# One cosine product between every four attention products in a graph-attention kernel

## The reference, cut to what matters

```
h     = relu(layernorm(x))
deg   = clip(adj.sum(axis=1), 1);  dis = deg ** -0.5
diff  = (dis[:, None] * adj * dis[None, :]) @ h - h
sim   = h @ h.T / (|h_i| |h_j|)
attn  = softmax(beta * sim * adj, axis=1)
out   = x + diff + sigmoid(alpha) * (attn @ h - h)
```

## Time and profile before

| | |
|---|---|
| median of three runs | 1919.48 us (1919.47 to 1920.07) |
| the profiled execution's own time | 1921.04 us |
| its span, first to last instruction | 1919.1 us |
| TensorE busy | 1827.4 us, 95% |
| ScalarE, GpSimd, VectorE busy | 1306.8, 1269.1 and 1226.5 us |
| mean granted TensorE clock | 0.991 |

### The profile page before, as it was taken

The page is one execution under the profiler, slowest core; times in us unless marked ns, Lnnn a source line. Parts: engine busy times, 40 slices in busy tenths (PEclk is TensorE's granted clock), DMA queues, the critical chain, the costliest instruction groups (busy, mean ns, idle before and its releaser), DMA issues.

```text
span 1919.1 us, 44747 instructions
## 1 busy us (share of the span) xinstructions
PE 1827.4 (95%) x19602; PEld 1408.7 (73%) x19602; DVE 1226.5 (64%) x1382; ACT 1306.8 (68%) x1262; POOL 1269.1 (66%) x792
## 2 busy tenths in 40 slices
PE   0489999999999999999999999999998999999998
PEld 0366777777777777777777777777777888888887
DVE  6887787787778778777877877787775210111111
ACT  7688898889889888988988898899887000000000
POOL 3099999999999999999999999999883000000000
PEclk9699999999999999999999999999999999999999
DMA  9639887767888877778888767888426755554530
GB/s 177 97 63 135 106 106 101 100 89 102 100 106 101 108 105 89 100 96 100 106 100 109 100 89 100 100 107 100 116 92 239 226 178 182 170 200 165 202 107 12
DMA packets 188455, 229.38 MB, mean 120 GB/s; under 512 B 9316, under 2 KB 164964, under 8 KB 183396
## 3 DMA queue, kind: packets, MB, share of 16 engines
q0 software_dynamic: 135168, 67.13, 45.1%
q1 hardware_dynamic: 25060, 144.71, 20.6%
q10 hardware_dynamic: 28032, 14.69, 3.0%
HBM read 352.32 MB, written 75.50 MB: 223 GB/s over the span
## 4 chain that ended last, share of the span: by engine, by line
PE 93%; ACT 3%; DVE 2%; issue 1%; POOL 1%; DMA 0%; SPq 0%; DVEq 0%; ACTq 0%
PE cos_ps L670 34%; PE top_ps L700 12%; PE top_ps L704 12%; PE cos_ps L726 12%; PE top_ps L726 12%; PE top_ps L702 12%; ACT arena L329 1%; ACT xe L353 0%; POOL hlo L278 0%; POOL ustage L287 0%; PE cos_ps L656 0%; DMA asb<-x_in 0%; DVE ustage L518 0%; DVE ptmp L489 0%; ACT xe L337 0%
## 5 line engine op out<-in xcount | busy, mean ns | idle before, releaser
L287 POOL TENSOR_TENSOR ustage<-xe,ustage 128x1024 f16<-128x1024 f32 x512 | 1094.7, 2142 | 155.3 <-ACT xe L410 148.2
L584 DVE TENSOR_TENSOR xe<-cos_ps,arena 128x1024 f32<-128x1024 f32 x512 | 627.0, 1225 | 286.2 <-PE cos_ps L670 191.5
L406 ACT ACTIVATE ustage<-xe,ebias,ab 128x1024 f16<-128x1024 f32 x512 | 635.3, 1241 | 132.2 <-DVE xe L584 128.8
L700 PE MATMUL top_ps<-h,ustage 128*128 128x129 f16 x4096 | 719.2, 220 | 6.2 <-POOL ustage L287 6.1
L704 PE MATMUL top_ps<-h,ustage 128*128 128x129 f16 x4096 | 718.9, 220 | 0.0
L702 PE MATMUL top_ps<-hlo,ustage 128*128 128x128 f16 x4096 | 718.4, 219 | 0.0
L410 ACT ACTIVATE xe<-xe,ebias,ab 128x1024 f32<-128x1024 f32 x512 | 628.6, 1228 | 5.5 <-POOL ustage L287 4.7
L700 PEld LDWEIGHTS top_ps<-h,ustage 128*128 128x128 f16 x4096 | 400.8, 98 | 75.6 <-POOL ustage L287 15.9
L702 PEld LDWEIGHTS top_ps<-hlo,ustage 128*128 128x128 f16 x4096 | 400.8, 98 | 56.6
L704 PEld LDWEIGHTS top_ps<-h,ustage 128*128 128x128 f16 x4096 | 400.8, 98 | 0.0
L559 DVE TENSOR_REDUCE top_ps<-arena 128x8 f32<-128x1024 uint16 x256 | 311.8, 1218 | 2.0 <-DMA arena<-adj_in_dram 2.0
(11 more groups left out here) (87 smaller groups left out, 1017.5 us busy)
## 6 DMA issues: line engine op xcount, KB each, us to landing
arena<-adj_in_dram POOLq DMA_DIRECT2D x256, 256.0 KB, 8.6
at_scratch<-arena SPq DMA_DIRECT2D x128, 512.0 KB, 3.3
arena<-at_scratch SPq DMA_DIRECT2D x26, 2048.0 KB, 8.9
xe<-at_scratch SPq DMA_DIRECT2D x6, 2048.0 KB, 8.5
h_scratch<-arena SPq DMA_DIRECT2D x4, 1024.0 KB, 7.6
arena<-h_scratch SPq DMA_DIRECT2D x2, 2048.0 KB, 8.8
ustage<-h_scratch ACTq DMA_DIRECT2D x16, 256.0 KB, 3.0
ptmp<-x_in ACTq DMA_DIRECT2D x64, 64.0 KB, 5.0
```

The costliest lines, as they stand in the source:

```text
L287: nc.gpsimd.tensor_tensor(elo[:, n % ES, :], ef[:, n % XS, :], ehi[:, n % ES, :], ALU.subtract).then_inc(elo_done, 1)
L406: nc.scalar.activation(ehi[:, n % ES, :], xm[:, n % XS, :], ACT.Exp, bias=ebias[:, 0:1], scale=ab[:, 1:2]).then_inc(ehi_done, 1)
L584: nc.vector.tensor_tensor(xm[:, n % XS, :], cos_ps[:, n % 2, :], at8[:, m % W, :, n % B], ALU.mult).then_inc(x_done, 1)
L700: nc.tensor.matmul(top_ps[:, bank, col:col + P + 1], head, h1[:, s, 0:P + 1], start=(first and t % 3 == 0), stop=final, skip_group_check=True)
```

## The change: what it does

`LAG` goes from 3 to 4. `cosines(n)` becomes `cosine(n, k)`, one of the six products, and `sums(n)` becomes `sums_begin(n)`, which holds the waits, and `sums(n, k)`, one of the 24. Within a unit, TensorE now issues one cosine product of unit n, then four sum products of unit n-4, six times over. The waits of the sums stand behind the first cosine product. The old arrangement (six, then 24) is kept for the first unit that sums into a new panel (n % 64 == 4, the unit that waits for `acc_copied`); units 0 to 3 have cosines alone and the last four iterations sums alone. Each product is the same as before, with the same operands and the same number.

```diff
-    LAG = 3
+    LAG = 4
...
-            def cosines(n):
+            def cosine(n, k):
...
-                if n >= 2:
+                m, q = k // 2, k % 2
+                if k == 0 and n >= 2:
                     pe.wait_ge(x_done, n - 1)
...
+                if k == 5:
+                    last.then_inc(cos_done, 1)
...
-            def sums(n):
-                s = tile_of(n % TILES // 16, n % 16 // B, n % B)
-                first, final = n % TILES == 0, n % TILES == TILES - 1
-                if first and n:
+            def sums_begin(n):
+                if n % TILES == 0 and n:
                     pe.wait_ge(acc_copied, n // TILES)
                 if n == UNITS - 6:
                     degrees()
                 pe.wait_ge(elo_done, n + 1)
...
             for n in range(UNITS + LAG):
-                if n < UNITS:
-                    cosines(n)
-                if n >= LAG:
-                    sums(n - LAG)
+                if n < LAG:
+                    for k in range(6):
+                        cosine(n, k)
+                elif n >= UNITS:
+                    sums_begin(n - LAG)
+                    for k in range(24):
+                        sums(n - LAG, k)
+                elif n % TILES == LAG:
+
+                    for k in range(6):
+                        cosine(n, k)
+                    sums_begin(n - LAG)
+                    for k in range(24):
+                        sums(n - LAG, k)
+                else:
+                    for k in range(6):
+                        cosine(n, k)
+                        if k == 0:
+                            sums_begin(n - LAG)
+                        for j in range(4):
+                            sums(n - LAG, 4 * k + j)
```

More of the change, by code:

```diff
@@ L660, in tiles_of @@
                 return uT[:, :].rearrange("d (ch w b p) -> d w b ch p", ch=CH, w=W, b=B)[:, w, b]
-            def cosines(n):
+            def cosine(n, k):
                 w0, b = panel_of(n // TILES)
-                s = tile_of(n % TILES // 16, n % 16 // B, n % B)
-                if n >= 2:
+                t = tile_of(n % TILES // 16, n % 16 // B, n % B)
+                m, q = k // 2, k % 2
+                if k == 0 and n >= 2:
                     pe.wait_ge(x_done, n - 1)
[L667 to L673, removed]
+                mine, src = ((uT_hi, uT_hi), (uT_hi, uT_lo), (uT_lo, uT_hi))[m]
+                last = nc.tensor.matmul(cos_ps[:, n % 2, q * HALF:(q + 1) * HALF].rearrange("p (ch i) -> p ch i", ch=CH),
+                                        mine[:, t * P:(t + 1) * P], tiles_of(src, w0 + q, b),
+                                        start=(m == 0), stop=(m == 2), skip_group_check=True)
+                if k == 5:
+                    last.then_inc(cos_done, 1)
             def degrees():
@@ L695, in sums @@
                     pe.wait_ge(hlo_ready, n // 4 + 1)
[L696 to L699, removed]
+            def sums(n, k):
+                s = tile_of(n % TILES // 16, n % 16 // B, n % B)
+                first, final = n % TILES == 0, n % TILES == TILES - 1
+                t, part = k // 3, k % 3
+                bank, col = t // 3, t % 3 * HS
+                head = ehi[:, n % ES, t * P:(t + 1) * P]
+                tail = elo[:, n % ES, t * P:(t + 1) * P]
+                if part == 0:
@@ L700, in sums @@
                     nc.tensor.matmul(top_ps[:, bank, col:col + P + 1], head, h1[:, s, 0:P + 1],
                                      start=(first and t % 3 == 0), stop=final, skip_group_check=True)
+                elif part == 1:
                     nc.tensor.matmul(top_ps[:, bank, col:col + P], head, hlo[:, s, :],
                                      start=False, stop=final, skip_group_check=True)
+                else:
                     last = nc.tensor.matmul(top_ps[:, bank, col:col + P + 1], tail, h1[:, s, 0:P + 1],
@@ L705, in sums @@
                                             start=False, stop=final, skip_group_check=True)
-                last.then_inc(attn_done, 1)
+                    if t == PT - 1:
+                        last.then_inc(attn_done, 1)
             pe.wait_ge(uT_copied, 2 * CH)
             for n in range(UNITS + LAG):
-                if n < UNITS:
-                    cosines(n)
-                if n >= LAG:
-                    sums(n - LAG)
+                if n < LAG:
[11 more added lines that the diff above has]
+                        sums(n - LAG, k)
+                else:
+                    for k in range(6):
[4 more added lines that the diff above has]
+                            sums(n - LAG, 4 * k + j)
```

## The result

| | before | after |
|---|---|---|
| median (ten runs each) | 1920.30 us | 1925.78 us |
| lowest and highest | 1919.47, 1922.08 | 1925.14, 1927.17 |
| ratio to before | | 1.0028, 95% interval 1.0018 to 1.0038 |
| span of the profiled execution | 1919.1 us | 1923.2 us |

The change makes the kernel 0.28% slower. The forecast was 1924.2 us and 4.7 us more than before; the medians differ by 5.5 us, the two profiled spans by 4.1 us. The forecast counted from a median of three runs before (1919.48 us); the ten runs here put before at 1920.30 us. So of the 1.6 us by which the measured time is above the forecast, 0.8 us lie in the time before.

The account below looks back on a forecast made before the run. TensorE was taken to bound the kernel, streaming almost without gaps from 180 us. Panel changes +5.1 us and leaving the GpSimd stretch -0.45 us gave +4.7 on 1919.48, so 1924.2 us; 8-in-10 range 1918.9 to 1928 us.

Parts of the forecast that it names:

- Item 1: TensorE's switches between cosine and sum products, ten more in each of 500 units: cost 0, bounds 25 us either way.
- switches cost: Rival, 3%: the first product behind a switch shows its weight load, 0.04 us, 100 us in all, giving 2024 us.
- A mixed stream is quicker: Rival, 7%: short products behind long ones lose gaps on TensorE, 6.5 us gained (1917.7 us), up to 31 us (1893).
- Item 2: In each unit the cosines and all that follows end 1.13 us later; three waits still hold, cost 0.
- The three waits: Cosines n+2 for mask n (1.38 us spare), exponential n for sums n-4 (1.14), sums n for GpSimd (2.28): cost 0.
- the mask comes too late: Rival, 8%: VectorE work delays masks and TensorE waits 0.1 us each fourth unit, 12.5 us, giving 1936.7 us.
- Item 3: At seven panel changes the copy queues behind unit 66's exponentials on ScalarE; TensorE loses 0.73 us more each, +5.1 us.
- S: Start of the six cosine products between a panel's last sum and the next's first; copy's data ready at S + 0.20.
- the copy stays in time: Rival, 12%: ScalarE reaches the panel copy by S + 0.20, below a cosine shift of 0.40 us; 1919.0 us.
- Item 4: Leaving the stretch to 180 us where GpSimd is full, all later masks come 0.45 us earlier: -0.45 us.
- Item 5: Start and end of the kernel: extra cosines fall into an existing wait, the chain behind the last mask is unchanged; cost 0.

Follow-up runs that it names:

- e1: The changed kernel with a finished panel's copy between the two exponentials of unit 66 instead of behind both: 1921.03 us, 1.0004 of before.
- e3: The changed kernel with LAG = 3 as before, so the interleaving alone: 1996.46 us, 1.0397 of before.
- e6: The changed kernel with each of a panel's three copies signalling on its own, so TensorE waits per bank: 1921.72 us, 1.0005 of before.
- e2: The kernel before with LAG = 4 alone, each unit still six cosine products and then 24 sum products: 1918.29 us, 0.9989 of before.
- e4: The changed kernel with two sum products instead of four between cosine products, the last 14 behind the sixth: 1921.62 us, 1.0008 of before.
- e7: The kernel before (lag of three, blocks) with a panel's copy moved behind the two exponentials of unit 66: 1943.07 us, 1.0121 of before.

## Why the prediction was right, point by point

*Item 1, switches, taken as 0 with bounds of 25 us.* Right: a unit is 2.65 us in both traces, and e1 has all the switches at 1.0004. The bounds were far too wide: they came from reading two switches alone. The rival "switches cost" is refuted by e1. "A mixed stream is quicker" is refuted by the same two readings.

*Item 2, the cosines 1.13 us later.* Right to 0.01 us along the whole chain. The three waits held in ordinary units, and e3 shows that the third holds only by the lag. The first did not hold at one place behind the start-up, which I had not looked at. Near 160 us VectorE waits for the adjacency rows of the third chunk, which a DMA brings. In the changed kernel, VectorE, and TensorE behind it:

```profile
160.48 1.23 DVE L559 TENSOR_REDUCE top_ps<-arena 128x8 f32<-128x1024 uint16 x1 [2.56 <-DMA arena<-adj_in_dram]
161.61 1.22 DVE L584 TENSOR_TENSOR xe<-cos_ps,arena 128x1024 f32<-128x1024 f32 x1
```

```profile
162.88 0.39 PE L670 MATMUL cos_ps<-uT_hi 128*128 128x512 f16 x1 [0.53 <-DVE xe L584]
```

Before, VectorE waited 1.97 us there and TensorE did not notice, since it had 2.51 us instead of 1.38 in hand. In the changed kernel this wait fell into the GpSimd stretch, where TensorE waits anyhow. In e1 it was longer:

```profile
161.23 1.23 DVE L559 TENSOR_REDUCE top_ps<-arena 128x8 f32<-128x1024 uint16 x1 [2.96 <-DMA arena<-adj_in_dram]
```

```profile
163.64 0.39 PE L670 MATMUL cos_ps<-uT_hi 128*128 128x512 f16 x1 [0.94 <-DVE xe L584]
```

So the rival "the mask comes too late" has its mechanism, at one place and not in each fourth unit: for 0.5 us in the changed kernel, 0.9 us in e1, and up to 1.2 us in the others (e6).

*Item 3, the panel change, +0.73 us each.* Right, with 0.69 for 0.73. The copy is at S + 0.93 as worked out; the load follows 1.17 us behind it and not 1.21, since the three copies took 1.12 us instead of 1.16. e1 takes the term away by moving the copy, e6 by shortening the wait, e2 by keeping the cosines together, e4 gives the intermediate value and e7 enlarges it. The rival "the copy stays in time" is wrong for the changed kernel, and its threshold is what e4 shows.

*Item 4, -0.45 us behind the GpSimd stretch.* Right in this trace. The first and the last mask of the changed kernel are

```profile
92.86 1.23 DVE L584 TENSOR_TENSOR xe<-cos_ps,arena 128x1024 f32<-128x1024 f32 x1 [1.77 <-PE cos_ps L670]
```

```profile
1457.51 1.22 DVE L584 TENSOR_TENSOR xe<-cos_ps,arena 128x1024 f32<-128x1024 f32 x1 [1.42 <-PE cos_ps L670]
```

The last is 4.16 us later than before; the first is 0.27 us earlier (93.13 before). 4.16 + 0.27 - 4.83 = -0.40 us is left for this item. In e1 the gain is there at first and goes at the DMA wait, where TensorE lost 0.94 us: counted from the first mask, the mask of unit 20 starts 0.42 us earlier than before, that of unit 40, behind the wait, only 0.05 us earlier. That is why e1 does not end below before. So this item came out as forecast in part by luck: how much of it is left depends on how long one DMA takes.

*Item 5, the ends.* Right: from the last mask to the end of the span there are 465.8 us before and 465.7 us after. In the other traces it is 465.5 to 465.9 us, with e4's 466.5 as the exception.

*The sum.* By the traces the change costs 4.83 - 0.40 = 4.4 us, less 0.27 that was gained before the first mask; 4.7 were forecast. The 0.27 need not come from the change: the first mask starts anywhere from 91.8 to 93.6 us in the nine traces. The medians say 5.5 us, within an interval of 3.5 to 7.3 us. The two profiled executions took 1921.04 and 1925.17 us, 4.1 us apart; the first lies 0.7 us above its kernel's median of ten and the second 0.6 us below its own, and that makes up the difference between traces and medians. Why executions of one kernel differ at all (before from 1919.1 to 1921.9 us, e4 from 1920.0 to 1925.8 us) is open. The start of the first mask and the DMA wait near 160 us, 1.9 to 3.4 us long in eight traces and absent in e3, may be among the reasons; no run singles them out. The granted clock ahead of the stage does not account for the first mask: from 60 to 91 us it was 0.56 to 0.64 in four traces (before, e1, e6, e7) and 1.00 in the five others, and the first mask starts at 91.8 to 93.2 us in the four and at 92.9 to 93.6 us in the five.

*The chances.* Those of the forecast and its four rivals add up to 98%; the other 2% belong to nothing that was named, and seem to be in the 4% for "faster".

## What to carry to other kernels

Where the bounding engine already streams without gaps, as here, another order moved only the times at which it hands work over; its own pace stayed at 2.65 us a unit. Follow the later hand-over (here 1.13 us) through every wait of every engine, also those that come once in 64 units: the ordinary ones had more room than that here, and the rare one did not. Where an engine's copy has to be finished before the bounding engine goes on, place it by when its data are ready (e1), or signal piece by piece (e6); either one brought the changed kernel from 1925.8 us to between 1921 and 1922. A longer lag in blocks, without the interleaving, was worth 2.5 us in the trace by itself.

## What the runs showed of the hardware that I had not expected

A pause of 2.2 us on TensorE cost more than itself: behind four of seven such pauses the granted clock fell (0.66 over the next 5 us at the second change), and those four cost 4.0 us each instead of 2.34 (e7). Behind the shorter pauses of the changed kernel (about 0.6 us by its waits), it stayed at 1.00. From 180 us on TensorE had been busy without a gap before each. Why four of the seven and not the others fell is not shown.
